# Expert blocks spread evenly through an edge-gathering stage, tiles planned four gathers late, and a chunk's first weights issued ahead of its rows

## The reference

```python
xw  = layernorm(x) @ W
msg = xw[src] * rsqrt(out_degree)[src][:, None]
agg = segment_sum(msg, dst)
x   = x + relu(agg * rsqrt(in_degree)[:, None] + b)
n   = layernorm(x)
p   = softmax(n @ Wr + br);  top_p, top_i = top_k(p, 2);  w = top_p / sum(top_p)
xe  = layernorm(n) * ln_g[e] + ln_b[e]                      # for each of 8 experts
y_e = gelu(xe @ W1[e] + b1[e]) @ W2[e] + b2[e]             # 256 -> 1024 -> 256
out = x + sum of w * y_e over the two chosen experts
```

## Time and profile before

| What | us |
|---|---|
| Median of 3 runs | 1953.3 |
| Lowest and highest | 1946.1, 1953.99 |
| The profiled execution, its own time | 1965.97 |
| Its span, first to last instruction | 1964.5 |
| PE, matmuls busy | 1244.9 (63%) |
| POOL busy | 1104.1 (56%) |
| DVE busy | 942.2 (48%) |
| ACT busy | 614.5 (31%) |

### The profile page before, as it was taken

One profiled execution on the slowest core, in us unless ns is written; L12 is line 12 of the kernel. 1 busy time (PEld: TensorE's weight loads), 2 busy tenths in 40 slices (PEclk: granted clock), 3 DMA queues, 4 the chain that ended last, 5 costly groups with the idle time before them and its releaser, 6 DMA issues.

```text
span 1964.5 us, 26622 instructions
## 1 busy us (share of the span) xinstructions
PE 1244.9 (63%) x9098; PEld 1030.0 (52%) x9098; DVE 942.2 (48%) x2432; ACT 614.5 (31%) x1218; POOL 1104.1 (56%) x1112
## 2 busy tenths in 40 slices
PE   0792564755357346884578538857872883778992
PEld 0792443534245135773467437645761772666892
DVE  0897543646434152545244524544553474554441
ACT  0946101102032003440344124414321452445660
POOL 2102776776766666666666666566665614563334
PEclk9999655656578567986799769978985996898996
DMA  4007665554464337753675367538644737778772
GB/s 150 8 1 237 219 227 187 180 188 136 143 212 141 96 94 254 230 176 96 226 258 164 105 210 234 186 121 283 209 135 161 252 122 244 252 261 255 229 238 25
DMA packets 147232, 350.99 MB, mean 179 GB/s; under 512 B 25768, under 2 KB 95946, under 8 KB 130712
## 3 DMA queue, kind: packets, MB, share of 16 engines
q1 hardware_dynamic: 86204, 205.79, 31.0%
q0 software_dynamic: 54528, 137.10, 23.9%
q10 hardware_dynamic: 6364, 6.40, 1.0%
HBM read 291.21 MB, written 59.89 MB: 179 GB/s over the span
## 4 chain that ended last, share of the span: by engine, by line
PE 33%; issue 20%; DVE 14%; another core or an unknown queue 12%; DMA 10%; ACT 5%; POOL 3%; SPq 1%; DVEq 1%; POOLq 0%; ACTq 0%
PE ps L1183 10%; PE ps L1198 8%; PE ps L1097 6%; DMA out<-gt,toks 5%; PE ps L1064 3%; ACT h L1048 2%; PE ps L1135 2%; DMA idx<-in_dst 2%; POOL out L833 2%; PE ps L1128 1%; DVE ohl L1244 1%; PE ps L1108 1%; DMA gt<-zt,srcI 1%; DMA S<-ys,cidx 1%
## 5 line engine op out<-in xcount | busy, mean ns | idle before, releaser
L786 POOL DMA_INDIRECT gt<-zt,srcI x832 | 831.6, 1000 | 440.0 <-issue 192.0
L1183 PE MATMUL ps<-xe,w1b 128*128 128x256 f16 x2688 | 370.2, 291 | 115.5 <-issue 56.6
L1097 PE MATMUL ps<-gt,S 128*128 128x257 f16 x1664 | 331.3, 335 | 126.0 <-issue 62.7
L1183 PEld LDWEIGHTS ps<-xe,w1b 128*128 128x128 f16 x2688 | 276.9, 104 | 177.6 <-issue 69.2
L1198 PE MATMUL ps<-w2b,hT 128*128 128x256 f16 x2688 | 335.6, 282 | 37.1 <-issue 24.2
L1048 ACT ACTIVATE h<-ps,cb 128x256 f32<-128x256 f32 x448 | 227.4, 558 | 379.3 <-remote 182.6
L1583 DVE SCALAR_TENSOR_TENSOR hT<-h,cb,hT 128x512 f16<-128x512 f32 x224 | 167.9, 750 | 323.7 <-ACT hT L1052 253.8
L1097 PEld LDWEIGHTS ps<-gt,S 128*128 128x128 f16 x1664 | 225.5, 155 | 186.2 <-issue 116.0
L1198 PEld LDWEIGHTS ps<-w2b,hT 128*128 128x128 f16 x2688 | 269.9, 101 | 85.4 <-issue 47.2
L1052 ACT ACTIVATE hT<-h,cb 128x512 f16<-128x512 f32 x224 | 161.7, 722 | 7.3
L803 POOL DMA_INDIRECT xs<-xrow,slI x98 | 99.3, 1014 | 81.4 <-ACT xrow L1030 43.8
(11 more groups left out here) (249 smaller groups left out, 1217.1 us busy)
## 6 DMA issues: line engine op xcount, KB each, us to landing
w1b<-ws SPq DMA_DIRECT2D x56, 1024.0 KB
w2b<-ws SPq DMA_DIRECT2D x56, 1024.0 KB
ws<-w2b SPq DMA_DIRECT2D x16, 1024.0 KB
xb<-xs SPq DMA_DIRECT2D x56, 258.0 KB
gt<-zt,srcI POOLq DMA_INDIRECT x832
ys<-yb SPq DMA_DIRECT2D x36, 256.0 KB
w1b<-in_L_ffn_W SPq DMA_DIRECT2D x8, 1024.0 KB
hT<-in_L_ffn_W SPq DMA_DIRECT2D x8, 1024.0 KB
```

Of the source, the lines that this page charges most:

```text
L786: e.indirect_dma_start(out=gt[:, i % NG, :], out_offset=None, in_=zt, in_offset=bass.IndirectOffsetOnAxis(ap=srcI[:, c, r:r + 1].bitcast(u ...
L1097: inst = e.matmul(PS[r % 2][:, 0:257], S[:, r % NS, :, c], gt[:, i % NG, part * 257:part * 257 + 257], start=(c == 0 and part == 0), stop= ...
L1183: inst = e.matmul(UP[n % 2][:, z * BS:(z + 1) * BS], w[:, l, kk, j * 128:(j + 1) * 128], xe[m % 2][:, k, kk, :], start=(kk == 0 and l == 0 ...
```

## The change

Three things. The planner's `BEHIND` counts four gathers, not eight. In chunks 0 to 4 (`BLOCKS[m][0] < LAST - 2`) a block's first `up` is not placed until 19.0 planned us (`PACE`) after that of the block before, as long as edge tiles are left; until then only `down`s may be placed. And SP's step `ld` is cut into `ldw` (the weights) and `ldx` (the rows), in that order; for a chunk's first block `ldw` is placed as soon as the chunk's block table has been read (`regs`, through `early`), while its rows are still being scattered. For the planner, rows of chunks 0 to 4 land 11.0 us after their step, not 7.0.

```diff
@@ -160,11 +160,11 @@
 
     order = []
     clock = {"PE": 0.0, "DVE": 0.0, "ACT": 0.0, "POOL": 0.0}
-    s = {"now": 0.0, "bank": 0.0, "held": {}, "free": {}, "turned": 0, "used": 0, "norms": -1, "nT": 0, "nW": 0, "hh": 0, "xr": 0, "placed": 0, "tabled": 0, "read": -1, "routed": -1, "loaded": 0, "fetched": False, "asked": False, "given": 0}
+    s = {"now": 0.0, "bank": 0.0, "held": {}, "free": {}, "turned": 0, "used": 0, "norms": -1, "nT": 0, "nW": 0, "hh": 0, "xr": 0, "placed": 0, "tabled": 0, "read": -1, "routed": -1, "loaded": 0, "fetched": False, "asked": False, "given": 0, "listed": -1, "begun": 0.0}
     later, sent = [], {}
-    HAND, SLACK = 0.5, 0.5
-
-    BEHIND = [1.25 * min(8, (R * CT - 1 - i) // 2) for i in range(R * CT)]
+    HAND, SLACK, PACE = 0.5, 0.5, 19.0
+
+    BEHIND = [1.25 * min(4, (R * CT - 1 - i) // 2) for i in range(R * CT)]
 
     def emit(kind, arg, costs, ready):
         order.append((kind, arg))
@@ -199,12 +199,21 @@
         def have(m):
             return m < NB and BLOCKS[m][0] <= s["routed"]
 
+        def early(m):
+
+            if m not in weighted and s["listed"] >= BLOCKS[m][0] and len(behind) < 2:
+                weighted.add(m)
+                order.append(("ldw", m))
+
         def load(m):
             if have(m) and s["loaded"] == m:
-                order.append(("ld", m))
+                if m not in weighted:
+                    weighted.add(m)
+                    order.append(("ldw", m))
+                order.append(("ldx", m))
                 s["loaded"] += 1
                 low[m] = None
-                landed[m] = max(s["now"], sent[BLOCKS[m][0]]) + 7.0
+                landed[m] = max(s["now"], sent[BLOCKS[m][0]]) + (11.0 if BLOCKS[m][0] < LAST - 2 else 7.0)
 
         def turn(m):
             end = emit("turn", m, (("PE", 0.55), ("ACT", 0.65)), s["now"])
@@ -227,7 +236,7 @@
                 gives.append(m)
 
         landed = {}
-        turned = set()
+        turned, weighted = set(), set()
         behind = collections.deque()
 
         def next_down():
@@ -245,6 +254,7 @@
 
         for m in range(NB):
             while not have(m):
+                early(m)
                 yield next_down()
             if s["loaded"] == m:
                 load(m)
@@ -257,6 +267,10 @@
                 turn(m)
             while low[m] is None or low[m] > s["now"]:
                 yield next_down()
+
+            while at["tile"] < n and BLOCKS[m][0] < LAST - 2 and s["now"] < s["begun"] + PACE:
+                yield next_down()
+            s["begun"] = s["now"]
             for q in range(4):
                 while not (clock["PE"] <= s["now"] + SLACK and clock["ACT"] <= s["now"] + 1.5):
                     yield False
@@ -373,6 +387,8 @@
                     s["fetched"] = True
                 if kind == "sent":
                     sent[arg] = max(s["now"], clock["POOL"]) + 2.0
+                if kind == "regs":
+                    s["listed"] = arg
                 if kind == "routed":
                     s["routed"] = arg
                 chain.at = end + 2.0 if kind == "cg" else s["now"] if kind == "xs" else end
@@ -932,31 +948,31 @@
                         at = e.value_load(endI[0:1, ex:ex + 1], min_val=0, max_val=SPARE * BS)
                         e.dma_start(xs[bass.ds(at, BS), :].rearrange("(n p) c -> p n c", p=128),
                                     blank[:, :].unsqueeze(1).to_broadcast([128, BS // 128, XW])).then_inc(s_blank, 16)
-                elif kind == "ld":
+                elif kind == "ldw":
                     m = arg
-                    c, k = BLOCKS[m]
-                    if m == 0 or BLOCKS[m - 1][0] < c:
-                        e.wait_ge(s_ek, c + 1)
-                        for z in range(NSC):
-                            e.wait_ge(s_sc[z], sent(c, z))
-                        if c == LAST:
-                            e.wait_ge(s_blank, 16 * (E + 1))
                     if m == 0:
                         e.wait_ge(s_wst[0], 16 * E)
                         e.wait_ge(s_wst[1], 16 * E)
                         e.wait_ge(s_wlo, 3 * E)
                     if m not in regs:
                         where(m)
-                    ex, ro = regs[m]
+                    if m >= 2:
+                        e.wait_ge(s_h, 4 * (m - 1))
+                    e.dma_start(w1b[m % 2][:, :], ws[0][bass.ds(regs[m][0], 1), :, :].squeeze(0)).then_inc(s_w1[m % 2], 16)
+                elif kind == "ldx":
+                    m = arg
+                    c, k = BLOCKS[m]
+                    if m == 0 or BLOCKS[m - 1][0] < c:
+                        for z in range(NSC):
+                            e.wait_ge(s_sc[z], sent(c, z))
+                        if c == LAST:
+                            e.wait_ge(s_blank, 16 * (E + 1))
                     if NX <= m < M0 + NX:
                         e.wait_ge(s_xT, m - NX + 1)
                     elif m >= M0 + NX:
                         e.wait_ge(s_y, m - NX - M0 + 1)
-                    e.dma_start(xb[m % NX][:, :, :], xsb[bass.ds(ro, 1), :, :].squeeze(0).rearrange("(s p) c -> p s c", p=128)
+                    e.dma_start(xb[m % NX][:, :, :], xsb[bass.ds(regs[m][1], 1), :, :].squeeze(0).rearrange("(s p) c -> p s c", p=128)
                                 ).then_inc(s_xb[m % NX], 16)
-                    if m >= 2:
-                        e.wait_ge(s_h, 4 * (m - 1))
-                    e.dma_start(w1b[m % 2][:, :], ws[0][bass.ds(ex, 1), :, :].squeeze(0)).then_inc(s_w1[m % 2], 16)
                 elif kind == "ld2":
                     m = arg
                     if m >= 2:
```

## The result

The changed kernel takes 1995.3 us in the median, the kernel before in the same comparison 1952.0: a ratio of 1.020, with a 95% interval of 1.016 to 1.024. The profiled execution took 1999.4 us (span 1997.9), 33.4 us more than that of before.

A forecast was written before the change was run, and what follows sets the result against it. POOL was taken to bound the edge stage, except in bursts, where PE has too much work per tile. Terms -94 - 12 + 2 + 3 = -101 us, off the median 1953.3, gave 1852 us; range 1803 to 1940.

The forecast's parts named there:

- The budget: Edge stage, 205 to 1571 us: POOL waits 194.7 us, 117 of them in the block bursts of chunks 0 to 4.
- So PE takes 32.4 us too long for the tiles that it is given there: Chunk 2's burst, blocks 10 to 16: PE took 121.1 us for 69 tiles that POOL could gather in 88.7.
- The pace: Bursts of chunks 0 to 4: tiles moved in at 0.34 us of PE each cut POOL's waits, -94 us.
- the ring's help: In bursts, PE may stall four more slots (5.1 us) before POOL stands; with 4.3 already there, 9.4 a chunk.
- The bare chain: A block's first down waits on its own last up: 0.9 us a block uncovered, 5.3 in six blocks.
- Four gathers late: Edge-stage waits outside those bursts, 77 us: the same four slots were to save 12, bounds 0 and 50.
- Weights ahead: Chunk starts: an earlier transfer shortens the third up's 10.24 us stall, by 0 to 10 us a chunk, taken as 3.
- Rows behind weights: Tail: rows issued after weights cost 0 to 1 us a block in 16 blocks, taken as +2, upper end +16.
- An unchanged tail: After the last gather: the tail was assumed to stay at some 393 us.
- A: Rival: PE still bounds the paced stretches, without the ring helping; 32 us gained, 3 lost, 1924 us; chance 0.16.
- C: Rival: spreading work lowers PE's clock in bursts; below 0.76 the change loses, 2003 us at 0.70; chance 0.09.
- D: Rival: PE's lateness comes from ACT, DVE and semaphores whatever the order; POOL's waits return, 1950 us; chance 0.05.

The follow-up runs named there:

- ring8: Kernel before, order unchanged, but a gather at most 8 tiles ahead of TensorE, not 16: 1976.7 us against 1967.1, ratio 1.0046.
- loads_alone: The change with its pace set to 0 and tiles planned eight gathers late again, only the loads changed: 1957.4 us against 1952.4 before, ratio 1.0027.
- no_pace: The changed kernel with pace 0 instead of 19 us, loads and four gathers late kept: 1975.8 us against 1952.4 before, ratio 1.0123.
- denser10_edge: Kernel before with blocks' ups and downs planned cheaper, so packed closer, only while edge tiles are left: 1940.8 us against 1954.9, ratio 0.9926.

## Why the prediction was wrong, by its steps

**The budget was right, its reading was not.** 194.7 us of waits, 117 of them in bursts: the changed kernel has 217.7, and by the same subtraction 32.9 in chunk 2's stretch alone. The step that failed is "So PE takes 32.4 us too long for the tiles that it is given there". The rows showed that PE took that long; that it *needed* it was inferred. The earlier trace rows had PE busy for 118 of 154 us there, and the earlier trace rows a stall of 10.24 us. Through most of it POOL went on gathering, until 954.6, and then it stood, too:

```profile
958.98 0.94 POOL L786 DMA_INDIRECT gt<-zt,srcI  x1 [4.38 <-remote]
```

What the runs showed in place of want of throughput is waiting: with the pace PE is idle for 95 of 446 us of its steps, and with plain copies for gathers the same steps take 300 us, not 373. I took the stall for a small matter of the loads (3 us a chunk), and the burst for want of throughput.

**The pace (-94, with the ring's help and the weights).** The size of the tile was the error that carried all: 0.34 us is PE's busy time, but in steps the 45 tiles that the change adds cost (430.8 - 372.6) / 45 = 1.29 us each, as much as POOL needs to gather them. So nothing could be gained by giving tiles to a step. Alone the pace costs 12 us. The bare chain of 0.9 us a block, added by hand, did come: by the two groups above PE stands 34 us longer ahead of the `down`s, 1.1 us for each of the 30 paced blocks.

**Four gathers late: -12, and 9.4 a chunk of help from the ring.** Alone it costs 1.8%, about 35 us. The cushion was hardly worth anything: eight slots less cost 9 us in all. And the price that I named, PE meeting gathers that haven't landed, was put at nothing ("Hidden by POOL's own pace"); the change has 147.5 us of it, against 28.9, though ring8 shows that such waits, when short, cost little. I had not asked what else the plan's lateness places: it also places the scatters in POOL's queue and the last stores in SP's. "Some are waits for routing data, which a freer ring doesn't shorten" was the right thought, but they grew (36 us at the scatters of the edge stage, against 9). How much of the 1.8% is each of these stays open.

**Weights ahead (-3 a chunk).** They brought nothing that can be measured (loads_alone 0.9994 to 1.0061). The stall was not theirs: in no_pace the weights of block 10 went out 26 us before its first `up`, and the third `up` still waited 16.0 us.

**Rows behind weights (+2).** This step was right. In the tail SP issues the weights at 1902.02, the rows behind them, and PE turns the block 8.83 us after the weights, exactly as in the earlier trace rows and as for its neighbours; no turn of the tail waits for its rows but that of the first block (7.84 us, 6.17 before):

```profile
1902.02 0.33 SPq L961 DMA_DIRECT2D w1b<-ws  x1
1902.54 0.38 SPq L974 DMA_DIRECT2D xb<-xs  x1
```

```profile
1910.85 0.60 PE L1183 MATMUL ps<-ident,xb 128*128 128x128 f32 x4
```

The upper end of 16 us, which the prediction drew from the Trainium skill's rule on ring order ("DMA: Bandwidth & Descriptors", Queues, rings and completion order), did not come: loads_alone lies between -1 and +12 us. The Trainium skill says there only that descriptors are taken up in ring order, and also that a later one may finish its write before an earlier one; "must wait out the whole megabyte" was my reading. Whether the rows did wait out the megabyte can't be seen, since the turn wasn't waiting for them.

**An unchanged tail.** It failed too: 407.9 us, not 393. The chain is in the rows above (last store, gathering of results, gives). The store comes later because the plan now has eight writes, 13.15 us of SP's time, ahead of it; the other 7 us, behind the first `give`, stay open.

**The rivals.** A had the sign of its steps ("steps of 22 us or more at an unchanged clock are A": they are 22.7 us on the mean, the clock a little lower), but priced them as a gain of 32, and its reason was PE's throughput again. (Its sum takes off 3 us for routing and rows, where the forecast itself had 2 and 3; with 5 it is 1926.) C named the right outcome by the wrong mechanism: its threshold was a clock under 0.76, and the stretches have 0.83 to 0.85. Still the clock moved its way: in the steps of chunk 1 it is 0.95 before, 0.90 with the pace and 0.96 in denser10_edge. The Trainium skill ("TensorE: Matmul & The Clock Gate", HAM oscillation — how this bites in real kernels) describes a kernel that waits between short pieces of matmul work and starts them at half clock, and advises to put the work together; the direction agrees with the pace and with denser10_edge, but no run here separates the clock from the late results. What no rival had is that the wait grows with the tiles that are moved in; D came nearest ("POOL's waits come back in the longer stretches"), and had it at no change, not at a loss.

## What to carry to other kernels

Before moving work onto an engine because it is "too slow there", ask whether it is dense there: busy 118 of 154 us is an engine that waits, and its busy time per piece isn't what another piece costs. A cheap test is to take the suspected neighbour away (here: plain copies for gathers) with the order unchanged, and a second to change the size in both directions; the reverse of the edit was the gain. And a planner's number that is meant for one queue places the others, too: with 16 slots, eight late was the best of four, eight and twelve, and both others moved POOL's scatters and SP's last store, which a list of every queue's order would have shown beforehand.
